# Attention scores as plain float32 matmuls on two 64-row tiles, without stacked parts, in a new unit order

## What is computed

```python
mod = (_silu(L0_c) @ L0_wmod).reshape(32, 6, 1, -1)       # sa, ca, ga, sb, cb, gb
h = _layernorm(x) * (1 + ca) + sa
q, k, v = h @ Wq, h @ Wkv[:, :1024], h @ Wkv[:, 1024:]    # 16 heads of 64
s = einsum('bhid,bhjd->bhij', q * 64 ** -0.5, k)
p = where(causal_mask, 0.0, exp(s - max(s)))              # the maximum is over the whole row
attn = (p @ v / (sum(p) + 1e-8)) @ Wo + bo
x = x + ga * attn
h = _layernorm(x) * (1 + cb) + sb
hidden = silu(q4(h) @ q4(w_gate).T) * (q4(h) @ q4(w_up).T)
x = x + gb * (q4(hidden) @ q4(w_down).T)
```

## Time and profile before

| | |
|---|---|
| median of 3 runs | 1399.65 us (1399.06 to 1401.82) |
| profiled execution | 1400.84 us |
| span of its core, first to last instruction | 1399.0 us |
| busy: TensorE, VectorE, ScalarE, POOL | 95%, 82%, 69%, 62% |
| mean granted clock of TensorE | 0.985 |
| moved by transfers | 227.99 MB, of which HBM read 21.94 MB |

### The profile page before, as it was taken

One profiled execution on the slowest core, in us unless ns is written; L12 is line 12 of the kernel. 1 busy time (PEld: TensorE's weight loads), 2 busy tenths in 40 slices (PEclk: granted clock), 3 DMA queues, 4 the chain that ended last, 5 costly groups with the idle time before them and its releaser, 6 DMA issues.

```text
span 1399.0 us, 37184 instructions
## 1 busy us (share of the span) xinstructions
PE 1322.9 (95%) x10194; PEld 1101.7 (79%) x10194; DVE 1145.8 (82%) x2821; ACT 960.9 (69%) x3269; POOL 866.3 (62%) x1582
## 2 busy tenths in 40 slices
PE   4899999999999999999999999999999999999993
PEld 2678888888887888888888888888888888888872
DVE  5678888888888888888888888888888888988874
ACT  2767677677667677767767767767776867777750
POOL 0546566676666766666666666666666666666663
PEclk9999999999999999999999999999999999999995
DMA  5767777777677767677777677766767776777730
GB/s 146 185 154 169 172 183 168 166 168 166 162 175 177 170 165 167 163 170 182 167 167 168 163 168 178 173 166 167 165 163 170 183 170 165 168 163 170 178 90 10
DMA packets 160941, 227.99 MB, mean 163 GB/s; under 512 B 27376, under 2 KB 90736, under 8 KB 160912
## 3 DMA queue, kind: packets, MB, share of 16 engines
q1 hardware_dynamic: 160912, 227.65, 68.6%
HBM read 21.94 MB, written 4.28 MB: 19 GB/s over the span
## 4 chain that ended last, share of the span: by engine, by line
DVE 45%; PE 33%; issue 12%; ACT 5%; SPq 2%; POOL 1%; DVEq 1%; DMA 1%; ACTq 0%; POOLq 0%
DVE neg_max L774 11%; PE ps_m L825 11%; PE ps_o L961 6%; PE ps_s L908 6%; DVE qk_parts L664 5%; PE ps_m L888 3%; DVE qy L61 3%; DVE amax L53 3%; DVE qm L65 3%; PE ps_s L917 3%; PE ps_t L804 3%; ACT probs L583 3%; DVE qm L64 3%; DVE xn L747 2%; DVE h_r L599 2%
## 5 line engine op out<-in xcount | busy, mean ns | idle before, releaser
L774 DVE TENSOR_REDUCE neg_max<-ps_s 128x2 f32<-128x512 f32 x512 | 349.7, 683 | 152.2 <-PE ps_s L908 145.3
L583 ACT ACTIVATE probs<-ps_s,neg_max 128x128 f32<-128x128 f32 (+1 forms) x1024 | 418.7, 428 | 25.4 <-PE ps_s L917 25.2
L456 POOL TENSOR_SCALAR probs<-probs,r_den 128x256 f32<-128x256 f32 (+1 forms) x768 | 379.0, 509 | 0.0
L454 POOL TENSOR_TENSOR probs<-probs,r_den 128x128 f32<-128x128 f32 x256 | 102.2, 399 | 410.7 <-DVE r_den L791 406.0
L908 PE MATMUL ps_s<-stack 128*128 128x256 f32 x2048 | 333.7, 289 | 4.1 <-DMA stack<-qk_parts 3.5
L908 PEld LDWEIGHTS ps_s<-stack 128*128 128x128 f32 x2048 | 286.2, 190 | 13.8 <-DMA stack<-qk_parts 4.5
L804 PE MATMUL ps_t<-ident,probs 128*128 128x128 f32 x1536 | 223.6, 276 | 7.8 <-POOL probs L456 7.5
L961 PE MATMUL ps_o<-probs_t,v 128*64 128x256 f32 (+1 forms) x2048 | 223.0, 339 | 0.1
L583 ACT ACTIVATION_READ_ACCUMULATOR probs<-ps_s,neg_max 128x1 f32 x1024 | 218.7, 214 | 0.0
L570 ACT COPY probs_t<-ps_t 128x384 f32<-128x384 f32 x160 | 76.7, 479 | 188.5 <-PE ps_t L804 188.5
L804 PEld LDWEIGHTS ps_t<-ident,probs 128*128 128x128 f32 x1536 | 172.4, 140 | 22.3 <-POOL probs L456 22.0
(11 more groups left out here) (109 smaller groups left out, 1960.0 us busy)
## 6 DMA issues: line engine op xcount, KB each, us to landing
stack<-qk_parts SPq DMA_DIRECT2D x512, 192.0 KB, 2.7
stack<-qk_parts SPq DMA_DIRECT2D x512, 128.0 KB, 2.7
stack<-qk_parts SPq DMA_DIRECT2D x512, 64.0 KB, 2.3
mod_a<-mod_rows SPq DMA_DIRECT2D x32, 256.0 KB, 3.8
x_in<-L_attn_x SPq DMA_DIRECT2D x32, 128.0 KB, 2.2
x_res<-L_attn_x SPq DMA_DIRECT2D x32, 128.0 KB, 2.2
out<-y_out SPq DMA_DIRECT2D x32, 128.0 KB, 1.9
mod_b<-mod_rows SPq DMA_DIRECT2D x32, 64.0 KB, 2.9
```

The costliest lines, as they stand in the source:

```text
L456: ins = nc.gpsimd.tensor_scalar(cols, cols, r_den[:, par, s:s + 1], 1.0, ALU.mult, ALU.mult)
L583: ins = nc.scalar.activation(probs[:, u % 4, h, t * P:(1 + 2 * t) * P], ps_s[:, scores_bank(u, h), t * N:t * N + (1 + t) * P], ACT.Exp, bi ...
L774: nc.vector.tensor_reduce(neg_max[:, par, 2 * h:2 * h + 2], ps_s[:, scores_bank(u, h), :].rearrange("p (t j) -> p t j", t=2), AX.X, ALU.ma ...
```

## The change

- Scores are four plain float32 matmuls a unit in place of eight on `F32R`. Each goes over the 64 rows of one head: head 0 lies in partitions 0 to 63 of `qk`, head 1 in 64 to 127, so that the two heads use two 64-row tiles of the array. No parts are made, and `stack`, `qk_parts`, VectorE's subtraction and the six transfers a unit are gone. ScalarE's one copy to `qk` is all that is left.
- `ps_s` has four banks, two a unit in turn; scores wait for the exponentials of unit `u - 2`. `ps_t` has one bank in place of two.
- VectorE takes one maximum a unit, over two banks, in place of two.
- The order in a unit is new: scores, values of `u - 3`, transposes of head 0, place a, transposes of head 1, place b, mask, place c, mask.
- `PLACES` is a new table; `wo` and `down` are cut in two halves each, and the hidden quantisation on VectorE and POOL is placed anew.
- The rounded half of h comes from ScalarE by a second activation; x is normalised by `scalar_tensor_tensor` in place of `tensor_scalar`.

```diff
-        ps_s = ctx.enter_context(nc.psum_tensor("ps_s", [P, 3, 512], F32))
-        ps_t = ctx.enter_context(nc.psum_tensor("ps_t", [P, 2, 512], F32))
+        ps_s = ctx.enter_context(nc.psum_tensor("ps_s", [P, 4, 512], F32))
+        ps_t = ctx.enter_context(nc.psum_tensor("ps_t", [P, 512], F32))
...
-        PT0_ON_ACT = (0, 1, 2, 3, 5)
+        PT0_ON_ACT = (1, 2, 3, 4, 6)
+        OT_LATE = (3,)
...
-            (0, "b"): ("xqt", 2, 0), (0, "c"): ("v", 0, 1), (1, "b"): ("gate", 2, 0), (1, "c"): ("up", 2, 0),
+            (0, "b"): ("v", 0, 1), (0, "c"): ("xqt", 2, 0), (1, "b"): ("gate", 2, 0), (1, "c"): ("up", 2, 0),
...
-                            nc.scalar.copy(qk_parts[:, k % 2, :, 0, :], ps_m[bank][:, :].rearrange("p (n j) -> p n j", n=2)
-                                           ).then_inc(qk_high, 1)
+                            nc.scalar.copy(qk[:, k % 4, :, :], ps_m[bank][:, :].rearrange("p (n j) -> p n j", n=2)
+                                           ).then_inc(qk_ready, 1)
...
-                            nc.scalar.activation(h_t[:, :], ps_m[bank][:, 0:N], ACT.Identity, bias=mod_t[:, 0, bass.ds(b, 1)],
-                                                 scale=mod_t[:, 1, bass.ds(b, 1)]).then_inc(ht_ready, 1)
+                            for h in (h_t, h_r[0]):
+                                nc.scalar.activation(h[:, :], ps_m[bank][:, 0:N], ACT.Identity,
+                                                     bias=mod_t[:, 0, bass.ds(b, 1)],
+                                                     scale=mod_t[:, 1, bass.ds(b, 1)]).then_inc(ht_ready, 1)
...
-                    if kind == "qk":
-                        dve.wait_ge(qk_high, UNITS * b + k + 1)
-                        nc.vector.tensor_tensor(qk_parts[:, k % 2, :, 1, :], ps_m[bank][:, :].rearrange("p (n j) -> p n j", n=2),
-                                                qk_parts[:, k % 2, :, 0, :], ALU.subtract).then_inc(qk_ready, 1)
...
+                        dve.wait_ge(s_full, UNITS * i + u + 1)
+                        nc.vector.tensor_reduce(neg_max[:, par, :],
+                                                ps_s[:, 2 * par:2 * par + 2, :].rearrange("p b (t j) -> p (b t) j", t=2),
+                                                AX.X, ALU.max, negate=True).then_inc(max_ready, 1)
...
+                def scores(u):
+                    pe.wait_ge(qk_ready, UNITS * i + u + 1)
+                    if has.after(u - 2):
+                        pe.wait_ge(exp_done, 16 * i + 2 * (u - 2) + 2)
...
+                    for t in range(2):
+                        for h in range(2):
+                            rows = slice(h * DH, (h + 1) * DH)
+                            mm = nc.tensor.matmul(ps_s[:, 2 * (u % 2) + h, t * N:(t + 1) * N],
+                                                  qk[rows, u % 4, 0, t * P:(t + 1) * P], qk[rows, u % 4, 1, :],
+                                                  start=(t == 0), stop=True, skip_group_check=True)
                     mm.then_inc(s_full, 1)
...
+                def probs_transposed(u, h):
+                    pe.wait_ge(probs_ready, 16 * i + 2 * (u - 2) + h + 1)
+                    if h == 1:
+                        pe.wait_ge(pt0_ready, UNITS * i + u - 1)
+                    elif has.after(u - 3):
+                        pe.wait_ge(pt1_ready, UNITS * i + u - 2)
```

More of the change, by code:

```diff
@@ L239, in adaln_block @@
         down_full = sem("down_full")
-        qk_high = sem("qk_high")
         qk_ready = sem("qk_ready")
@@ new lines, in body @@
+                    if has.unit(u - 3) and u not in OT_LATE:
+                        out_copy()
+                    if has.unit(u - 2) and u in PT0_ON_ACT:
+                        act.wait_ge(pt_full, 16 * i + 2 * (u - 2) + 1)
+                        nc.scalar.copy(probs_t[:, u % 2, 0, :], ps_t[:, 0:3 * P]).then_inc(pt0_ready, 1)
+                    shared_reads(u, "a")
+                    if has.unit(u - 2):
+                        act.wait_ge(pt_full, 16 * i + 2 * (u - 2) + 2)
+                        nc.scalar.copy(probs_t[:, u % 2, 1, :], ps_t[:, 0:3 * P]).then_inc(pt1_ready, 1)
@@ L592, in _ @@
+                    shared_reads(u, "b")
+                    if has.attn:
+                        exponentials(0)
+                    shared_reads(u, "c")
+                    if has.unit(u - 3) and u in OT_LATE:
+                        if has.prev:
+                            act.wait_ge(wo_full, 2 * i)
+                        out_copy()
+                    if has.attn:
+                        exponentials(1)
             iterations(act, body)
@@ L918, in mask, with values @@
                                      start=False, stop=True, skip_group_check=True).then_inc(masked, 1)
-                for u in range(UNITS):
-                    par = u % 2
+                def values(u):
+                    w = (u - 3) % UNITS
+                    pe.wait_ge(pt0_ready, UNITS * i + u - 2)
+                    pe.wait_ge(pt1_ready, UNITS * i + u - 2)
+                    if u >= 3:
+                        pe.wait_ge(v_ready, 4 * i + (4 if w >= UNITS // 2 else 2))
+                    if has.after(u - 4):
+                        pe.wait_ge(ot_ready, UNITS * i + u - 3)
+                    for n, (keys, q0) in enumerate(((0, 0), (1, P))):
+                        for h in range(2):
+                            head = (2 * w + h) * DH
+                            mm = nc.tensor.matmul(ps_o[h * DH:(h + 1) * DH, q0:N], v[:, keys, head:head + DH],
+                                                  probs_t[:, w % 2, h, (0 if n == 0 else N):(N if n == 0 else 3 * P)],
+                                                  start=(n == 0), stop=(n == 1), skip_group_check=True)
+                    mm.then_inc(o_full, 1)
@@ L922, in body @@
+                for u in range(UNITS):
+                    if has.attn:
+                        scores(u)
+                    if has.unit(u - 3):
+                        values(u)
+                    if has.unit(u - 2):
+                        probs_transposed(u, 0)
                     at_place(u, "a")
-                    if has.attn:
-                        pe.wait_ge(stacked[par], STACKED * i + UNIT_STACKED * (u // 2 + 1))
-                        scores(u, 0)
+                    if has.unit(u - 2):
+                        probs_transposed(u, 1)
@@ L927, in body @@
                     at_place(u, "b")
-                    if has.attn:
-                        if has.after(u - 1):
-                            pe.wait_ge(exp_done, 16 * i + 2 * (u - 1) + 2)
-                        scores(u, 1)
-                    if i_is(i, 0) and u == 2:
-                        pe.wait_ge(setup_dve, SETUP_ROWS)
-                    if has.unit(u - 2):
-                        g = (u - 2) % UNITS
-                        for h in range(2):
-                            pe.wait_ge(probs_ready, 16 * i + 2 * (u - 2) + h + 1)
-                            if has.after(u - 3):
-                                pe.wait_ge(pt1_ready if h else pt0_ready, UNITS * i + u - 2)
-                            for c in range(3):
-                                mm = transpose(ps_t[:, h, c * P:(c + 1) * P], probs[:, g % 4, h, c * P:(c + 1) * P])
-                            mm.then_inc(pt_full, 1)
```

213 lines of the change are left out of this document (77 added, 136 removed), and 6 rows, old and new, of the table PLACES.

## The result

| | before | after |
|---|---|---|
| median | 1399.65 us (1399.06 to 1401.82) | 1407.76 us (1407.34 to 1408.96) |
| span | 1399.0 us | 1405.9 us |
| busy: TensorE, VectorE, ScalarE, POOL | 95%, 82%, 69%, 62% | 95%, 69%, 71%, 60% |

The ratio is 1.0056, 95% interval [1.0042, 1.0071]: the changed kernel is slower by 0.6%, where the prediction had it faster by 1.2%. It lies in the predicted range, on the other side of no change.

What follows compares the result with a forecast made beforehand. TensorE was taken as nearly full (95% busy), the rest lost to waits for VectorE. Terms 26 - 69 + 29 - 2 = -16 from 1399.65 gave 1383 us, range 1345 to 1425 for 8 in 10.

Steps and rivals of the forecast that it cites:

- Score matmuls: Each unit's score block: four plain float32 matmuls, 0.87 us if heads run side by side, 1.74 one after another.
- the switch of the array's shape: Scores directly ahead of values: one shape switch more a unit, 0.18 us; with the scores +0.10 a unit, +26 us.
- I take half of 0.35: Extra switch priced at 0.18 us, half the 0.35 us read for going to the 64-wide shape and back.
- Waits that go: TensorE's waits, largely for VectorE, vanish with the subtraction, transfers and tighter score banks: -69 us, bound -25.
- The mask of unit 6: Largest single wait before: transposes to mask took 1.45 us where 0.66 would do, behind VectorE's maximum.
- the prediction's 39.3 us: TensorE's batch without waits before the change: 8 x 3.57 for units plus 10.73 of shared work.
- all 69 us of the old waits: TensorE's waits before the change: 2.1 us a batch over 32 batches, all expected to go.
- less work stands ahead of each maximum: VectorE: subtraction gone, 5.4 us a batch; hidden quantisation spread over units 1 to 4, less ahead of one maximum.
- Waits that come: Second head's transposes wait for the copy from the one bank: 0.9 us a batch, +29 us.
- the upper bound that I had given (1.9): Upper bound of the new waits: 1.9 us a batch, +60 us, if each copy is a further 0.12 us late.
- rival 2: Single transpose bank becomes the new wait at the second head's transposes in each unit: slower, about 1427 us; 15%.
- The ends of the program: Program's ends: the first scores need no transfer, -2 us.

Runs made afterwards that it cites:

- the run on the same rows: Changed kernel with both heads' scores computed from head 0's 64 rows, for timing only: 1622.8 us, one run.
- The best run: Changed kernel with step b between the heads' transposes, first head's copy always on ScalarE, and the cast back on VectorE: 1363.4 us, ratio 0.9747 to the kernel before.
- one statement moved on TensorE: Changed kernel with the shared step of place b put between the two heads' transposes: 1377.8 us, ratio 0.9845 to the kernel before.
- the copying engine: Changed kernel with ScalarE copying the first head's transposed probabilities in all eight units, VectorE in none: 1383.6 us, ratio 0.9882 to the kernel before.
- both 41: Changed kernel with step b between the heads' transposes and the first head's copy always on ScalarE: 1366.7 us, ratio 0.9765 to the kernel before.
- the run without the loop: Changed kernel with transposes in blocks of four and two, the last two in the free half of the values' bank: 1374.4 us, ratio 0.9824 to the kernel before.
- over all 128: Changed kernel with both heads' scores computed over all 128 rows, using no row tile, for timing only: 1560.3 us, one run.

## Why the prediction was wrong

*Score matmuls* and *the switch of the array's shape*: right. A block of 1.06 us against 1.05, and two tiles side by side, which the run on the same rows shows. "I take half of 0.35" came out too, at 0.19 us, but no row had shown the half: that is luck in part. Read from mask to values, the new scores cost TensorE 0.12 us a unit more than the old, for 0.10 predicted, 31 us for 26. By the Trainium skill ("TensorEngine Tiling (Array Packing)", Key Properties) a change of tiling mode drains the engine and different tiles work in parallel; the 0.19 us and the 0.86 us measured here agree with both.

*Waits that go*: right in kind. The mask of unit 6 no longer waits for its maximum, there is no transfer to wait for, and VectorE's share of the chain fell from 45% to 9%. By the prediction's 39.3 us and the measured 8 x 0.12 a batch without waits should take 40.3. The changed kernel less its 2.0 us of waits takes 39.9. The best run has 40.61 and about 0.6 of waits (0.2 and 0.1 at the masks of units 2 and 3, 0.18 and 0.14 behind masks of units 5 and 6), so 40.0. Both confirm the price of a batch within 0.4 us, and so all 69 us of the old waits did go. One part of the reasoning holds only while TensorE is slow: that less work stands ahead of each maximum did not keep the masks of units 2 and 3 from waiting once the gap was closed.

*Waits that come*: this is the step that failed, as a term mis-sized. It said "about 1.05 us from their start until the second head may go", and "the wait is near zero when the copying engine is free". The loop takes 1.21 us with ScalarE free, and the cover is 1.09, where I had 1.05 for both. The 0.16 us by which the loop is longer have two parts: the three transposes behind the tiled value block end 0.55 us after their start, where I had 0.49, and the two hand-overs take 0.04 us ahead of the copy and 0.14 behind it, where I had 0.08 in all. The four units that I had at nothing wait 0.12 us each. The other four wait 0.36, 0.56, 0.36 and 0.28, for 0.15, 0.45, 0.15 and 0.15. In sum 2.0 us a batch in place of 0.9, 35 us; it lies just past the upper bound that I had given (1.9). The period confirms it within 0.4 us (41.93 against 40.3 + 2.0), and what the 0.4 us are I can't say.

This is rival 2, at a price between forecast and rival. Its rule was that at 0.17 us a unit the sum is 1427 us; measured beyond the forecast are (2.0 - 0.9) / 8 = 0.14. That it was the cause is shown and not only argued: one statement moved on TensorE gave 30 us back, the copying engine 24, both 41. Not all of the 65 us (32 x 2.0) came back in any run, because waits for VectorE's maxima and ScalarE's copies showed up in their place.

*The ends of the program*: -2 us predicted, and the head gave 11.1 back while the tail cost 4.2. In the head and tail the steps of neighbouring batches are missing; why they changed is not shown. Without the shorter head the changed kernel would be 1.4% slower and not 0.6%, so the steady part is worse than the total tells.

The sum, over the 29 steady periods: -0.54 us a batch forecast (41.44 to 40.9), +0.48 measured, a miss of 29.5 us; the ends took 6.6 of it back.

## What to carry to other kernels

When two uses of a buffer become one, write the loop down from rows (first write to end, hand-over, copy, hand-over) and compare it with the work between them before calling it hidden: here a cover 0.12 us too short in half of the units, and late copies in the others, cost 2.0 us in each of 32 batches, and moving one statement gave back nearly half of it. A wait that is removed uncovers the ones behind it, so a change should be priced together with the next two candidates for lateness; the run without the loop gave 1.0 us a batch (41.93 to 40.93), where the waits had been 2.0. And blocks that use the array in tiles belong side by side, because a trip back to the whole array costs (0.18 us a unit here).

## What the runs showed of the hardware

- Two 64-row tiles work side by side whatever the order in which their matmuls are issued (1407.8 and 1409.1 us, blocks of 1.06 and 1.07); what decides is only that they use different rows (1622.8 us where they don't; one run each of the last two kernels).
- Entering the row shape from the whole array cost 0.19 us, and three transposes put between two tiled blocks 0.18 us more than elsewhere (0.48 against 0.30). Rows to columns cost no more than whole array to columns: the last score record to the first value record took 0.31 us in both (the runs on the same 64 rows and over all 128).
- An operation of VectorE can take three times as long beside POOL. The normalisation of x moved from `tensor_scalar` to `scalar_tensor_tensor`, whose second tensor is a column repeated. Groups of VectorE in the changed kernel:

```profile
L689 DVE SCALAR_TENSOR_TENSOR xn<-x_in,mv,rstd 128x128 f32<-128x128 f32 x64 | 60.6, 985 | 5.1 <-POOL rstd L434 1.2
...
L689 DVE SCALAR_TENSOR_TENSOR xn<-x,mv,rstd 128x128 f32<-128x128 f32 x64 | 28.2, 479 | 1.2 <-POOL rstd L434 1.2
```

At the first place it went from 734 ns to 985, at the second from 719 to 479, so that nothing was won or lost in all (88.0 and 88.8 us). In both traces the few of these operations that have no instruction of POOL beside them take 0.34 to 0.35 us, whatever their kind; at the slow place of the changed kernel POOL works through operations of 0.8 to 0.9 us meanwhile, and they take 1.04 us. By the Trainium skill ("SBUF — State Buffer", SBUF: two separate sides) an operation of VectorE with two inputs in SBUF and one of GpSimd that reads SBUF exclude each other for a whole instruction. The 1.04 against 0.35 us agree with that; no run here separates it from other causes. In the changed kernel it lies beside TensorE's work and did not set the time. In the faster runs it begins to: the maximum of unit 3 stands right behind it, and the mask there waits for that maximum.
